# Gated stage: the three group sums of each step, and the quantising behind them, are placed one projection later

## The reference

```python
# gated memory (after a layer norm)
q, k, v, a, g = split(x @ w_in.T, 5)
q = q * rsqrt(mean(q*q over a head of 32) + 1.19e-7)
k = tanh(k);  a = clip(sigmoid(a + 2.0), 0.6, 0.9995);  u = k * v
# per chunk of 64 tokens:
prefix = cumprod(a);  acc = cumsum(u / max(prefix, 1e-6))
memory = prefix * (state + acc)
y = sigmoid(g) * (q * memory) + (1 - sigmoid(g)) * v
out = x + y @ w_out.T

# ternary weights of the feed-forward layer, groups of 64
scale = clip(mean(abs(w_group)), 1e-8)
w_hat = clip(round(w_group / scale), -1, 1) * scale
```

## Time and profile before

| | us |
|---|---|
| median of 3 runs | 2203.25 (2202.75 to 2207.26) |
| the profiled execution | 2203.24 |
| its span (first to last instruction) | 2201.4 |
| TensorE busy | 2031.9 (92%) |
| VectorE busy | 1279.8 (58%) |
| GpSimd busy | 888.4 (40%) |
| ScalarE busy | 854.9 (39%) |
| the 16 gated steps, 14.64 to 396.61 | 381.97 |

### The profile page before, as it was taken

One profiled execution on the slowest core, in us unless ns is written; L12 is line 12 of the kernel. 1 busy time (PEld: TensorE's weight loads), 2 busy tenths in 40 slices (PEclk: granted clock), 3 DMA queues, 4 the chain that ended last, 5 costly groups with the idle time before them and its releaser, 6 DMA issues. The chain is left out here.

```text
span 2201.4 us, 29717 instructions
## 1 busy us (share of the span) xinstructions
PE 2031.9 (92%) x11783; PEld 882.7 (40%) x11824; DVE 1279.8 (58%) x1836; ACT 854.9 (39%) x1304; POOL 888.4 (40%) x457
## 2 busy tenths in 40 slices
PE   7999999999999989999999999999997865999998
PEld 3444444444444443333434343333432222444444
DVE  5878778557664553545555555545556633475634
ACT  4535344244444224343343444343344341343331
POOL 4756576300000004656766765656666670000000
PEclk9999999999999999999999999999999886999999
DMA  7101011300000020000000000000000003000001
GB/s 228 35 29 34 29 34 34 129 1 0 1 1 1 25 46 1 16 1 24 7 15 15 11 20 11 20 1 15 1 15 1 10 1 115 1 1 20 17 3 39
DMA packets 68808, 55.55 MB, mean 25 GB/s; under 512 B 36608, under 2 KB 55040, under 8 KB 68416
## 3 DMA queue, kind: packets, MB, share of 16 engines
q1 hardware_dynamic: 61760, 41.07, 6.4%
q10 hardware_dynamic: 6912, 12.59, 1.9%
HBM read 43.02 MB, written 10.62 MB: 24 GB/s over the span
## 5 line engine op out<-in xcount | busy, mean ns | idle before, releaser
L1556 POOL TENSOR_TENSOR b_total<-b_total,b_prob 128x2048 f32<-128x2048 f32 (+3 forms) x160 | 515.5, 3222 | 357.1 <-ACT b_prob L1503 352.3
L1619 DVE TENSOR_REDUCE b_maxima<-psum 128x2 f32<-128x1024 f32 (+3 forms) x384 | 350.1, 954 | 436.3 <-PE psum L1349 247.9
L195 PE MATMUL psum<-hT,W 128*128 128x512 f16 x2048 | 450.2, 381 | 11.5 <-DMA W<-ternary 7.5
L1503 ACT ACTIVATE b_prob<-psum 128x1024 f32<-128x1024 f32 (+3 forms) x320 | 228.3, 765 | 283.4 <-PE psum L1384 200.9
L195 PEld LDWEIGHTS psum<-hT,W 128*128 128x128 bf16 x2048 | 201.0, 98 | 257.2 <-issue 9.5
L588 PE MATMUL psum<-hT,a_win 128*128 128x512 f32 x640 | 290.8, 597 | 2.6 <-DVE a_parts L880 1.2
L1343 PE MATMUL psum<-b_kT,b_qT 32*128 32x512 f32 (+3 forms) x1536 | 179.8, 535 | 38.7 <-ACT b_prob L1503 29.9
L1371 PE MATMUL psum<-b_qT,b_kT 32*128 32x512 f32 (+3 forms) x1536 | 181.3, 541 | 29.6 <-DVE b_maxima L1619 27.1
L588 PEld LDWEIGHTS psum<-hT,a_win 128*128 128x128 f32 x640 | 119.3, 191 | 129.7 <-issue 128.2
L1533 POOL MEMSET b_mask<- 128x128 f32 x1 | 0.2, 205 | 357.2 <-POOLq L420 357.2
L1343 PEld LDWEIGHTS psum<-b_kT,b_qT 32*128 32x128 f32 x1536 | 64.8, 184 | 177.8 <-issue 159.3
(11 more groups left out here) (192 smaller groups left out, 2903.5 us busy)
## 6 DMA issues: line engine op xcount, KB each, us to landing
a_parts<-in_w_guT ACTq DMA_DIRECT2D x32, 256.0 KB, 2.8
ternary<-W SPq DMA_DIRECT2D x1, 6144.0 KB, 18.1
a_win<-in_w_inT SPq DMA_DIRECT2D x20, 256.0 KB, 7.2
a_parts<-in_w_pT ACTq DMA_DIRECT2D x16, 256.0 KB, 2.6
b_lamT<-lam_rows SPq DMA_DIRECT2D x32, 128.0 KB, 2.7
W<-ternary SPq DMA_DIRECT2D x8, 512.0 KB, 7.5
out<-x SPq DMA_DIRECT2D x4, 1024.0 KB, 4.2
x<-in_x SPq DMA_DIRECT2D x3, 1024.0 KB, 8.0
```

The lines of the kernel that those rows point to most:

```text
L195: last = pe.matmul(self.bank[m % 2 * 2 + part], self.W[:, k * 2 * HID + col:k * 2 * HID + col + P], self.hT[:, at:at + BLK], start=(k + ha ...
L1503: act.activation(held(u, s)[:, 2 * a:2 * a + 2, off:BLK], pair_banks(("score", u, s, a))[:, :, off:BLK], ACT.Exp, scale=SCALE).then_inc(ex ...
L1556: pool.tensor_tensor(acc, acc, held(u, s)[:, :, off:BLK], ALU.add).then_inc(summed, 1)
L1619: dve.tensor_reduce(maxima[u % 2][:, :].rearrange("p (h q c) -> p h q c", h=HPT, q=QT)[:, 2 * a:2 * a + 2, qt, kc], pair_banks(("row", u, ...
```

## The change

TensorE's group sums and VectorE's quantising are put at later places in the lists of both engines. The list of ScalarE and that of GpSimd stay as they are, and so does the work of each instruction.

- `group(3s)` moves from behind projection 0 to behind projection 1 and the head squares.
- `group(3s+1)` moves from behind projection 2 to behind projection 3 and the spread.
- `group(3s+2)` moves from behind projection 4 to behind projection 0 of the next step; the last one stands after the loop.
- `quantise(3s+2)` moves from the end of step `s` to behind `finish(s)` (and `normal_rows`) in step `s+1`; `quantise(3s)` moves from there to behind the reciprocal (L921); `quantise(3s+1)` moves from behind L927 to between L946 and L949.
- The statistics of a "mid" norm get a wait of their own for the additions of its block.

```diff
--- before.py
+++ after.py
@@ tensor engine
             for s in range(NSTEP):
                 project(s, 0)
-                group(NP * s)
+                if s:
+                    group(NP * s - 1)
                 project(s, 1)
                 head_squares(s)
+                group(NP * s)
                 project(s, 2)
-                group(NP * s + 1)
...
                 project(s, 3)
                 spread(s)
+                group(NP * s + 1)
...
                 project(s, 4)
-                group(NP * s + 2)
+            group(PIECES - 1)
@@ vector engine
             def normal_stats(g):
                 kind, blk = of(g)
                 b = g % 2
+                if kind == "mid":
+                    dve.wait_ge(out_added, (blk + 1) * TPB)
...
-                quantise(NP * s)
+                if s:
+                    quantise(NP * s - 1)
 
                 dve.wait_ge(sq_summed, s + 1)
...
                 dve.reciprocal(inv_q[:, :], mean[:, :]).then_inc(inv_ready, 1)
+                quantise(NP * s)
...
                 dve.sem_inc(dve_took, 1)
-                quantise(NP * s + 1)
...
                 settle()
+                quantise(NP * s + 1)
                 dve.wait_ge(spread_done, s + 1)
                 dve.tensor_tensor(prefix[:, :], bank[4], q_sb[:, :], ALU.mult).then_inc(q_scaled, 1)
...
-                quantise(NP * s + 2)
                 if s in STATS_IN:
                     normal_stats(STATS_IN[s])
+            quantise(PIECES - 1)
             finish(NSTEP - 1)
```

## The result

| | before | after |
|---|---|---|
| median, us | 2203.65 (6 runs) | 2241.93 (2240.89 to 2245.28, 6 runs) |
| ratio | | 1.0172 (95%: 1.0159 to 1.0185) |
| span of the profiled execution | 2201.4 | 2241.8 |
| first instruction of the feed-forward layer on TensorE | 396.61 | 436.54 |

The change costs 38 us. The forecast said slower, by 17.5 us to 2221; the time is inside the range of 2208 to 2243, but the size is off by more than a factor of two.

A forecast was written before the change was run, and what follows sets the result against it. TensorE paces the gated steps, with 20.9 us idle. Waits 34.3 plus clock 6.7 make 41.0 against 24.6 before, +16.4; with +1.1 at the end +17.5, so 2221 us, 8-in-10 range 2208 to 2243.

The forecast's parts named there:

- The clock term: TensorE matmuls at lower clock behind seven waits of 3 us and more: together 6.7 us, between 0 and 12.
- 34.3 us: Sum of TensorE's new waits for bank 5 ahead of group(3s), over twelve gated steps.
- D: Time on VectorE from L940 of one step to the end of the next step's L880 for piece 3s-1.
- D - 10.55: TensorE's new wait ahead of group(3s) behind a plain step, in us; behind a turn step D - 11.0.
- I take the middle: VectorE's relief from GpSimd contention set between nothing and every two-operand SBUF instruction running at 0.69 us.
- the one case in this trace agrees: Step 6 before: a 3.00 us TensorE wait, then a 5.30 us projection, taken to support the skill's repeated-gap rule.
- The end of the stage: From L940 of step 15 to L281: one more quantising, +1.4 less 0.3 of relief, +1.1 us; group(47)'s wait hidden.
- GpSimd gives nothing back: Rival: D stays as measured before, reliefs of 25 us over twelve steps are lost, 2246 us; chance 0.17.
- GpSimd is out of the way: Rival: VectorE's L946, finish and rows run at 0.69 us each, waits fall by about 11, 2210 us; chance 0.13.
- ScalarE becomes the wait: Rival: ScalarE's piece(3s+1) waits for late GpSimd, up to 1 us in some ten steps, 2231 us; chance 0.07.
- Faster: Rival: L880 is done before TensorE reaches group(3s), all 24.6 us go and 1.1 come, 2180 us; chance 0.05.
- The signs of being wrong: Bank waits under 20 us or ahead of projection 3, or over 3 us of change behind the gated steps.

The follow-up runs named there:

- e2: Changed kernel with group(3s) alone put behind projection 2 on TensorE, VectorE's order unchanged: 2201.4 us.
- e7: Changed kernel with the quantising of piece 3s-1 ahead of the rows of a turn step, still behind finish(s-1): 2230.6 us.
- e8: Changed kernel with the head squares behind projection 2 instead of ahead of group(3s): 2255.6 us.
- e4: Changed kernel without the first three of GpSimd's four instructions per piece, so the ternary weights differ: 2211.6 us.
- e3: Changed kernel with matmuls nobody reads in front of group(3s), as long as the waits there: 2226.7 us.
- e6: Changed kernel with about half of each wait filled by matmuls nobody reads: 2240.1 us.
- e1: Changed kernel with the quantising of piece 3s-1 put ahead of finish(s-1) on VectorE: 2219.1 us.
- e5: Kernel of e2 with group(3s) also behind the first two turned tiles in the six turn steps: 2195.1 us.

## Why the prediction was right and wrong

In short: the direction, the new wait and its place were right. What failed is the size of two terms of the sum. The clock term, "together 6.7", came to 15.4, and the waits, "34.3 us", came to 41.1. Smaller misses make up the rest.

**The bound.** Right: TensorE paces the stage, nothing behind it changed (1805.3 against 1804.8 us), and what the kernel could give back was the idle time.

**The new wait and its place.** Right. The forecast said one large wait per step, behind the head squares, for the quantising behind finish, none behind an out step, steps 2 and 6 the longest. All twelve are there (42.8 us with the one at the end), and steps 5, 9 and 13 have none. The rule (the wait is D - 10.55 behind a plain step, D - 11.0 behind a turn step) holds with the measured D: step 12, 13.46 - 10.55 = 2.91 against 2.87; step 2 below. It holds in e2 too, where D and the asking place both moved: step 3 has D 16.51, less 11.0 and the 3.65 us of projection 2, which makes 1.86, and the wait is 1.85. e2, e7 and e8 moved either end of it and the time followed.

TensorE in step 2 of the kernel after, where VectorE released the bank at 73.24 (72.56 + 0.68):

```profile
73.39 0.58 PE L597 MATMUL psum<-a_parts,groupones 128*128 128x512 bf16 x1 [5.36 <-DVE a_parts L884]
73.77 5.54 PE L588 MATMUL psum<-hT,a_win 128*128 128x512 f32 x8
```

D was 57.41 to 73.24 = 15.83, so 5.28 us, and the wait is 5.36.

**The size of D (wrong, about 7 us of waits).** The step "I take the middle" took 25 us of relief off D, since GpSimd would rest longer. Forecast and measured waits, in us, for steps 1, 2, 3, 4, 6, 7, 8, 10, 11, 12, 14, 15:

- forecast: 3.35, 5.75, 3.0, 1.0, 5.45, 3.2, 1.0, 3.5, 1.35, 1.85, 3.5, 1.35, sum 34.3
- measured: 3.23, 5.36, 3.61, 1.57, 5.73, 4.00, 1.57, 4.62, 1.97, 2.87, 4.62, 1.96, sum 41.1 (about 0.4 too much in steps 6, 10 and 14, where the group sum has no record)

Of those 25 us, 19.0 did come off (188.8 - 169.8), so the middle was a fair guess, a quarter too high. Steps 1 and 2, with the statistics in between, came out as said or shorter. Where there are no statistics GpSimd's piece now starts just ahead of L955 and covers the scan (1.79 us, before 1.46) and three of the four instructions of finish, so what L951 (was L946) and L949 gained in some steps was partly lost again. e4 shows what was at stake: 30 us.

**The clock (wrong, about 9 us).** The term (1.7 for each of two waits, 0.7 to 0.9 for each of five, "together 6.7") was sized on one slow stretch in the trace of before. By its own rates it would have been 6.9 at the least. Less the 1.7 that before paid it gave +5.0. Measured are +15.9 us of TensorE busy time, of which 2.2 are the start of the stage, so +13.7: nine stretches with 15.4 us, which is the full 1.7 for each. Rows show why it could not be read from the length of a wait. Step 4 and step 8 of the kernel after have the same wait of 1.57 us:

```profile
125.02 0.38 PE L597 MATMUL psum<-a_parts,groupones 128*128 128x512 bf16 x1 [1.57 <-DVE a_parts L884]
125.23 5.29 PE L588 MATMUL psum<-hT,a_win 128*128 128x512 f32 x8
```

```profile
235.22 0.38 PE L597 MATMUL psum<-a_parts,groupones 128*128 128x512 bf16 x1 [1.57 <-DVE a_parts L884]
235.44 3.59 PE L588 MATMUL psum<-hT,a_win 128*128 128x512 f32 x8
```

Behind the one, the projection takes 5.29 us, behind the other 3.59. Steps 1, 2, 3, 4, 6, 7, 10, 12 and 14 have a slow stretch, 8, 11 and 15 have none, although their waits are 1.6 to 2.0 us as well; every wait of 2.87 us and more has one. The kernel before had 15 waits of 0.2 to 3.7 us and one stretch, and it was not the longest wait that had it. That one, in step 2, was not looked at in the forecast:

```profile
70.78 1.03 PE L550 MATMUL psum<-ident,a_t 128*128 128x128 f32 x8 [3.72 <-DVE a_parts L880]
71.64 3.60 PE L588 MATMUL psum<-hT,a_win 128*128 128x512 f32 x8
```

Even without the unrecorded group sum in it, this wait is longer than the 3.00 us of rows 8, and the projection behind it runs at full clock. So "the one case in this trace agrees" was a misreading: there were two cases, and they disagreed. The forecast's own sentence "waits of 1.2 us show no such stretch" was true and no ground for what waits of 3 us do. The rule of the Trainium skill that was set against the sum ("TensorE: Matmul & The Clock Gate", section "HAM oscillation — how this bites in real kernels"), that a gap repeated in every turn of a loop is paid in every turn, priced it 5 us higher. It was nearer. In the kernel after, all seven waits that it was applied to have their stretch, and e3 (15.2 us back by filling the waits) shows what they cost. In the kernel before, the wait of 3.72 us does not fit it. What e6 adds is that halving the waits gives back only 3 to 4 us of the clock.

**The end of the stage (small).** Forecast was +1.1 between the last L940 and L281, and the wait of group(47) hidden. From L945 of step 15 to L281 it is now 447.00 - 431.80 = 15.20 us, before 12.57, so +2.6:

```profile
431.80 0.17 DVE L945 TENSOR_SCALAR a_a_first<-psum 128x8 f32<-128x8 f32 x1 [3.23 <-ACT psum L749]
...
447.00 1.29 DVE L281 SCALAR_TENSOR_TENSOR a_win<-psum,a_win 128x512 f32<-128x512 f32 x2
```

The relief that was taken off there did not come: the scan takes 1.79 us where it took 1.46, the first instruction of finish 1.64 where it took 0.69. The wait of group(47) is 1.64 us and hidden, as forecast, since TensorE waits another 4.1 us for L281 behind it (3.3 before). In the windows above it counts as idle time of the gated stage all the same. In the turn steps 6, 10 and 14 another 1.2 us go on transposes that wait for the low halves (L872), which the sum left out.

**The sum again.** Idle +24.1 where +11.4 was forecast (34.3 less 22.9), clock and start of the stage +15.9 where +5.0, the rest +0.5 where +1.1: 40.5, within 0.1 the difference of the spans, against 17.5. The 12.7 us that the idle term lacks are, within 0.3, 6.8 of waits in the twelve steps, 1.6 ahead of group(47), 1.2 for the low halves, and 2.8 from the base: the sum took the waits of before as 24.6 less the slow stretch, 22.9 us, where the rows of before have 20.1 for the bank.

**The rivals.** "GpSimd gives nothing back" (2246, 0.17) was the nearest to the time, but it reached its figure by waits alone: the measured waits (41.1) lie about a quarter of the way from the forecast's 34.3 to its own, 25 us more, and the clock did the rest. "GpSimd is out of the way" is answered by e4. "ScalarE becomes the wait" did not occur in the changed kernel (in e2 it begins to): TensorE has no wait for it in the stage but that of 0.8 us at its start, which before has too. "Faster" needed a D under 10.5, and no step that waits has one; the smallest is 12.69, step 4.

**The signs of being wrong.** The forecast named three: waits under 20 us, waits ahead of projection 3, a change of over 3 us behind the stage. None came, and yet it was off by 21 us. No sign asked for the size of the clock term.

What stays open is what decides whether a wait brings a slow stretch: waits of 1.57 us do in one step and not in another, and one of 3.72 us did not. e8 rules out one idea (the squares ahead of it), no more.

## What to carry to other kernels

When a producer is reached through a single buffer, what counts is how late the consumer asks and how much the producer has queued ahead of it; work out the loop from release to release for both orders, as its rule was exact here (D - 10.55), given the D that was then measured. But D is no constant where a third engine slows the producer: when e2 took the waits away, D went back up by 17 us over twelve steps. Then look for the next demand in the same loop, since taking one away (e1) can leave the wait standing under another name. And price a new wait on the matrix engine with its slow clock behind it: here 24 us of added idle time came with 14 us of added slow clock. Filling or removing the waits brought that back; halving them brought back only 3 to 4 us.

## What the runs showed of the hardware that was not expected

- Idle stretches of TensorE of 1.0 to 2.7 us ahead of the group sums (e6) cost about 12 us of clock, where those of 1.6 to 5.7 us cost 15. Filled, they cost none (granted clock 1.00, 2226.7 us).
- The length of an idle stretch alone does not say whether slow matmuls follow: 3.72 us without (before, step 2), 1.57 us with (after, step 4).
- The second scan, with two SBUF operands, takes 1.22 us beside an idle GpSimd (step 0 of before) and 1.79 us when one GpSimd instruction starts beside it, and this even in e4, where GpSimd has a single instruction per piece (91.12 above).
- The first two projections of the stage take 7.1 us in some executions and 8.8 to 9.5 in others, with the same order up to there.
- With the same instructions throughout, the places of the group sum and the head squares alone span 60 us, from 2195.1 (e5) to 2255.6 (e8).
